# A two-layer metaformer kernel: the experts of group g+2 issued ahead of the second experts of group g, stages spread over more slots, and the weight broadcast cut into four pieces

## What is computed

```python
x = x + L0_conv(_ln_c(x), ...)     # state-space mixer of one image
t = t + L0_ffn(_ln_t(t), ...)      # 8 experts, hidden 128, top 2
x = x + L1_conv(_ln_c(x), ...)     # divisive normalisation, 3x3 taps + channel mix
t = t + L1_ffn(_ln_t(t), ...)      # 8 experts, hidden 256, top 2
```

## Time and profile before

| | |
|---|---|
| median of 3 runs | 746.52 us (745.37 to 746.63) |
| profiled execution | 745.84 us, of which the span is 744.1 us and 1.7 us lie around it |
| busy: TensorE matmul (PE) | 566.3 us, 76% of the span |
| weight load (PEld) | 276.6 us, 37% |
| VectorE (DVE) | 437.4 us, 59% |
| ScalarE (ACT) | 372.7 us, 50% |
| GpSimd (POOL) | 245.7 us, 33% |
| chain that ended last | PE 40%, DVE 27%, ACT 11%, DMA 8%, issue 7%, POOL 6% |

### The profile page before, as it was taken

The page is one execution under the profiler, slowest core; times in us unless marked ns, Lnnn a source line. Parts: engine busy times, 40 slices in busy tenths (PEclk is TensorE's granted clock), DMA queues, the critical chain, the costliest instruction groups (busy, mean ns, idle before and its releaser), DMA issues.

```text
span 744.1 us, 10005 instructions
## 1 busy us (share of the span) xinstructions
PE 566.3 (76%) x3778; PEld 276.6 (37%) x3778; DVE 437.4 (59%) x810; ACT 372.7 (50%) x454; POOL 245.7 (33%) x217
## 2 busy tenths in 40 slices
PE   2645675579868995999768986998589968976677
PEld 1242253325423442445224532454244523432333
DVE  3255347454777569574967487756865495546412
ACT  2214322565446655575548554764557564644432
POOL 2020243122523344342442342434434243423103
PEclk9999875799989999899989998999899997989688
DMA  4501400515014500641052401450055005320140
GB/s 66 101 0 43 87 0 0 109 35 104 1 32 98 116 0 15 130 90 27 15 112 52 83 14 49 82 116 1 17 114 114 3 15 115 85 46 0 25 91 28
DMA packets 27838, 41.47 MB, mean 56 GB/s; under 512 B 11792, under 2 KB 19088, under 8 KB 27792
## 3 DMA queue, kind: packets, MB, share of 16 engines
q1 hardware_dynamic: 27152, 38.75, 25.4%
q0 software_dynamic: 640, 2.10, 0.9%
HBM read 38.22 MB, written 2.62 MB: 55 GB/s over the span
## 4 chain that ended last, share of the span: by engine, by line
PE 40%; DVE 27%; ACT 11%; DMA 8%; issue 7%; POOL 6%; SPq 1%; POOLq 0%; DVEq 0%; ACTq 0%
PE yP L863 11%; PE hP L847 11%; DMA WB<-w_scratch 6%; DVE nacc L1149 4%; PE sA L773 3%; PE sA L786 3%; PE sA L780 2%; PE sC L876 2%; ACT H L690 2%; ACT L574 2%; POOL stat_b L494 2%; DVE xsplit L979 2%; DVE xnrm L976 2%; DVE xcen_b L976 2%; PE sA L759 2%
## 5 line engine op out<-in xcount | busy, mean ns | idle before, releaser
L690 ACT ACTIVATE H<-hP,b 128x1024 f32<-128x1024 f32 x192 | 211.0, 1113 | 111.1 <-PE hP L847 108.4
L863 PE MATMUL yP<-H,w 128*64 128x512 f32 x768 | 208.9, 626 | 21.9 <-DVE ACC L1193 14.3
L847 PE MATMUL hP<-xT,w 128*64 128x512 f16 x1536 | 215.7, 406 | 10.6 <-ACT H L690 10.5
L552 POOL TENSOR_TENSOR ACC<-ACC,YW 128x512 f32<-128x512 f32 x96 | 125.4, 1310 | 212.6 <-DVE YW L1193 212.5
L847 PEld LDWEIGHTS hP<-xT,w 128*64 128x64 f16 x1536 | 83.2, 115 | 139.0 <-issue 74.1
L1193 DVE SCALAR_TENSOR_TENSOR YW<-yP,b,WB 128x512 f32<-128x512 f32 x96 | 71.4, 744 | 30.2 <-PE yP L863 30.1
L863 PEld LDWEIGHTS yP<-H,w 128*64 128x64 f32 x768 | 54.1, 143 | 61.7 <-issue 30.6
L1149 DVE SCALAR_TENSOR_TENSOR nacc<-PAD,taps,nacc 128x528 f32<-128x528 f32 x56 | 52.7, 941 | 1.7
L1193 DVE SCALAR_TENSOR_TENSOR ACC<-yP,b,WB 128x512 f32<-128x512 f32 x32 | 23.1, 745 | 41.7 <-DMA WB<-w_scratch 41.7
L1207 DVE TENSOR_TENSOR X<-sC,X 128x256 f32<-128x256 f32 x32 | 13.5, 423 | 53.9 <-PE sC L876 53.9
L876 PEld LDWEIGHTS sC<-fold,ACC 128*128 128x128 f32 x256 | 32.4, 198 | 25.6 <-issue 19.1
(11 more groups left out here) (144 smaller groups left out, 728.4 us busy)
## 6 DMA issues: line engine op xcount, KB each, us to landing
WB<-w_scratch SPq DMA_DIRECT2D x32, 1024.0 KB, 10.1
X<-in_x SPq DMA_DIRECT2D x8, 256.0 KB, 12.0
out<-X POOLq DMA_DIRECT2D x8, 256.0 KB, 2.8
H<-in_L_ffn_W SPq DMA_DIRECT2D x2, 512.0 KB, 6.7
H<-in_L_ffn_W SPq DMA_DIRECT2D x2, 256.0 KB, 4.2
w<-in_L_ffn_W SPq DMA_DIRECT2D x1, 512.0 KB, 5.2
w_scratch<-wTs SPq DMA_DIRECT2D x16, 32.0 KB, 1.8
w<-in_L_ffn_W SPq DMA_DIRECT2D x1, 256.0 KB, 4.4
```

Of the source, the lines that this page charges most:

```text
L552: pool.tensor_tensor(ACC[l][:, cols], ACC[l][:, cols], YW[:, u % 4, :], ALU.add).then_inc(summed, 1)
L690: nc.scalar.activation(H[:, s % RING, :], hP[s % 2][:, :], ACT.Gelu, bias=b1[l][:, e * ch + c:e * ch + c + 1], scale=1.0 / WS)\
L847: mm = nc.tensor.matmul(hP[s % 2][b * C:(b + 1) * C, hf * HALF:(hf + 1) * HALF], w1[l][:, sp, w, b * C:(b + 1) * C], xT[l][g % 2][:, hf * ...
L863: mm = nc.tensor.matmul(yP[hf][a * C:(a + 1) * C, :], w2[l][:, (2 * j + a) * ch + c, :], H[:, (2 * ch * j + 2 * c + a) % RING, hf * HALF:( ...
```

## The change

- Moe(0, g) moves 24 slots ahead of where it stood relative to moe(1, g): a round is now moe(0, g+2) and moe(1, g). Before the rounds there are two stretches of 24 slots with first experts alone. The last two groups' second experts follow one another without first experts between them.
- The cd steps are spread over more slots (`turn_d` from 15 to 20, `send` from 19 to 25), and all start two slots later after their moe(0, g). The ab tables keep their numbers.
- `X3` gets a third buffer. Moe(1, 6) accumulates in `ACC0` instead of `ACC1`.
- The read of the weights is cut into four pieces, one for each expert pair, of two transfers of 256 KB, each with its own semaphore. A piece waits only for the units of that pair in the previous group. For the second experts the pieces are issued in slots of their own. VectorE waits for a pair's piece ahead of each pair.

```diff
+DEPTH = 2
 PE_AT = dict(
-    cd=dict(turn_c=4, pool0=4, turn_u=11, turn_d=15, gate=16, send=19),
-    final=(12, 14, 24, 26))
+    cd=dict(turn_c=5, pool0=6, turn_u=13, turn_d=20, gate=22, send=25),
+    final=(13, 16, 24, 26))
 ...
 def moe_start(layer, g):
-    return SLOTS * (g - 1) if layer == 0 else SLOTS * g + E
+    if layer == 0:
+        return SLOTS * (g - DEPTH)
+    if g + DEPTH < GROUPS:
+        return SLOTS * g + E
+    return moe_start(1, g - 1) + E * CHUNKS[1]
 ...
 def cd_start(g):
-    return moe_start(0, g) + E * CHUNKS[0] + LAG + 2
+    return moe_start(0, g) + E * CHUNKS[0] + LAG + 4
 ...
+            def spread_piece(l, g, j):
                 if g >= 1:
-                    sp.wait_ge(scaled, 8 * (POS[(l, g - 1)] + 1))
+                    sp.wait_ge(scaled, 8 * POS[(l, g - 1)] + 2 * j + 2)
                 for a in range(2):
-                    src = scratch[l][i].rearrange("(j a) n -> a j n", a=2)[a]
-                    sp.dma_start(WB[l][a * C:a * C + C, :, :], src.partition_broadcast(C)).then_inc(w_in[l][i], 16)
+                    sp.dma_start(WB[l][a * C:a * C + C, j, :],
+                                 scratch[l][g % 2][2 * j + a:2 * j + a + 1, :].partition_broadcast(C)
+                                 .rearrange("c a n -> c (a n)")).then_inc(w_in[l][j], 16)
 ...
                 if k == "send":
                     spread_weights(1, g)
+                    spread_piece(1, g, 0)
+                elif k in ("piece1", "piece2", "piece3"):
+                    spread_piece(1, g, int(k[-1]))
```

More of the change, by code:

```diff
@@ L63 @@
             sums_b=30, turn_b=31, top2=35, send=36),
-    cd=dict(sums_c=1, turn_c=4, norms=9, sums_d=11, turn_d=14, top2=17, send=18),
+    cd=dict(sums_c=1, turn_c=5, norms=11, sums_d=16, turn_d=20, top2=23, send=25),
     final=NO_FINAL)
@@ L68 @@
             centre_b=29, sums_b=30, norm_b=31, top2=35, weights=35),
-    cd=dict(centre_c=1, sums_c=1, norm_c=3, pool0=5, pool1=6, pool2=7, pool3=7, turn_u=10, centre_d=10,
-            sums_d=12, norm_d=14, top2=17, weights=18),
-    final=(12, 13, 24, 27))
+    cd=dict(centre_c=0, sums_c=1, norm_c=3, pool0=7, pool1=8, pool2=9, pool3=10, turn_u=14, centre_d=15,
+            sums_d=16, norm_d=18, top2=23, weights=24),
+    final=(13, 16, 24, 26))
 POOL_AT = dict(
     ab=dict(sums_a=7, norm_a=9, state=26, y_sums=28, sums_b=29),
-    cd=dict(sums_c=1, norm_c=2, scale=8, sums_d=12),
+    cd=dict(sums_c=1, norm_c=2, scale=12, sums_d=16),
     final=NO_FINAL)
@@ L77 @@
     ab=dict(decay=22, send=35),
-    cd=dict(send=21),
+    cd=dict(send=26, piece1=30, piece2=34, piece3=38),
     final=NO_FINAL)
@@ L136, in build_metaformer @@
         n += E * CHUNKS[m[0]]
+    ACC_OF = {m: 0 if m[0] == 0 or GROUPS - m[1] in range(2, DEPTH + 1) else 1 for m in ORDER}
+    ACC_BEFORE = {}
+    for i in range(2):
+        users = [m for m in ORDER if ACC_OF[m] == i]
+        ACC_BEFORE.update(zip(users[1:], users))
     with ExitStack() as ctx:
@@ L193, in build_metaformer @@
         X2b = sb("X2b", [P, T, C])
-        X3 = [sb(f"X3_{i}", [P, T, C]) for i in range(2)]
+        X3 = [sb(f"X3_{i}", [P, T, C]) for i in range(3)]
         X4 = [sb(f"X4_{i}", [P, T, C]) for i in range(2)]
@@ L281, in build_metaformer @@
         w_out = [[sem(f"w_out{l}_{i}") for i in range(2)] for l in range(2)]
-        w_in = [[sem(f"w_in{l}_{i}") for i in range(2)] for l in range(2)]
+        w_in = [[sem(f"w_in{l}_{j}") for j in range(PAIRS)] for l in range(2)]
         x2b = count("x2b", 1)
@@ L457, in ab @@
                     spread_weights(0, g)
+                    for j in range(PAIRS):
+                        spread_piece(0, g, j)
             def cd(g, k):
```

24 lines of the change are left out of this document (12 added, 12 removed).

## The result

The changed kernel takes 756.20 us in the median of four runs (755.18 to 757.23); the kernel before, on the same chip, 745.94 (742.31 to 746.63). The ratio is 1.0159, with a 95% interval from 1.0123 to 1.0196. The profiled execution took 755.29 us, of which the span is 753.5. I had forecast 739 and a gain.

The account below looks back on a forecast made before the run. TensorE was taken as the nearest bound, with 13.3 us of waits a round. The terms 66.7 + 58 + 70 + 407 + 55 + 80 gave a span of 737 us, and with run overhead 739 us, range 718 to 757.

Parts of the forecast that it names:

- the full round: Round of moe(0, g+2) and moe(1, g): 80.4 us less 7.2 saved plus 8.2 new, so 81.4 us.
- second stretch: Stretch with moe(0, 0) alone: shrinks from 68.61 to 58 us, mainly because the first weight piece lands 7 us earlier.
- the two last parts: After the full rounds: 24 slots with moe(0, 7) and moe(1, 5), 55 us; moe(1, 6), moe(1, 7) and the end, 80.
- what goes: Waits removed or shortened in a full round at yP, `mix`, `turn_d` and `send`: 7.2 us saved.
- The third stretch: New 24 slots with moe(0, 1) beside ab(2) and half of cd(0): 70 us, between 62 and 76.
- the wait is 4.1 instead of 1.54: At `turn_b` in a full round: only three slots remain after `mix_out`, adding 2.6 us of wait.
- Ahead of `Vs` now stand a `final` half and layer norm d, 144.30 to 146.18, 1.9 us: At `state` in a full round: TensorE waits 2.4 us for `Vs` instead of 0.57, adding 1.9.
- so +1.9 more: Behind the `turn_b` wait in a full round: TensorE runs at 1.2 GHz, costing 1.9 us more.
- The break-even: Round length R at which 329.7 + 5R equals the old span: 82.9 us, against 81.4 forecast.
- The third rival: In a full round, six taps become late and TensorE waits at `turn_u`: R = 86, 762 us; chance 0.22.
- The second: Rival at the start: weight pieces land no earlier, second stretch stays at 68, time 751 us; chance 0.08.
- The table loads: On ScalarE: twelve more loads of 1.28 us, some 2 us a round, counted only within the `turn_u` wait.

Follow-up runs that it names:

- runs with filled waits: Changed kernel plus matmuls with overwritten product ahead of the waits at `state` and `turn_b`: 734.25 us; with ten more at `send`: 725.89 us.
- the depth alone: Changed kernel with the cd and `final` tables of before, keeping two groups of depth and the four weight pieces: 727.07 us, ratio 0.9809.
- mixed tables: Changed kernel with old places for `turn_c`, channel mix and first taps, later ones for the rest, layer norm d behind `Vs`: 738.34 us, ratio 0.9944.
- depth and filled `send`: Changed kernel with the old cd and `final` tables, plus 23 matmuls with overwritten product in the wait at `send`: 717.01 us, ratio 0.9647.
- the filled `send`: Kernel before with only the four weight pieces, plus 23 matmuls with overwritten product in the wait at `send`: 709.09 us, ratio 0.9542.

## Why the prediction was wrong

**The direction failed on one term, the full round.** The parts, forecast and measured: second stretch 58 and 62.5, third 70 and 69.7, five rounds 407 and 422.4, the two last parts 55 + 80 and 54.8 + 77.5. The differences are +4.5, -0.3, +15.4 and -2.7; together 16.8, which is the span of 753.5 less the 736.7 that the terms of the forecast add up to. I had written that the round decides, from R = 82.9 on; it is 84.5 in the mean. The time of 756.2 lies just inside the stated range, on the side to which I gave a chance of 0.30.

**Right in the round:** what goes. No wait is left at `mix`, `turn_d` or the yP block for `YW`; `send` waits 2.69 us where I said 2.8. `turn_u` waits 1.89 (1.8 forecast) for `zT`. Gone are 7.3 us, where I had 7.2.

**The third stretch came out right by luck.** I built it as 58 for the nearest stretch and 12 of additions. The nearest stretch measured 62.5, so the additions were 7.2: two errors of some 4.5 us cancel.

**Wrong in size: the step "the wait is 4.1 instead of 1.54" at `turn_b`.** It is 5.21. I took the chain of before and gave it back 0.9 us, without asking what GpSimd does beside it in the new order. One VectorE row was held by an `ACC` addition before as well; now `X2b` runs there too and the two hold two rows. Moving `X2b` away gave back 0.95 us, nearly the whole of the error of 1.1.

**Wrong in size: the step "Ahead of `Vs` now stand a `final` half and layer norm d, 144.30 to 146.18, 1.9 us" at `state`.** The wait is 4.22 us instead of 2.4. The rows were the right ones, but I took their price of 1.9 us from the stretch with first experts alone, where GpSimd adds nothing beside them. In the full round before, the same three rows took 3.9 us (307.69 to 311.58), as they do in the changed kernel (394.02 to 397.90). These 2.0 us more cover the whole error of 1.8. Moving layer norm d away brought the wait to 2.45, not to 0.57; the two `zdt` rows then took 2.0 us more beside GpSimd's additions.

**Wrong in kind: the step "so +1.9 more", one stretch at 1.2 GHz.** I priced the clock behind `turn_b` only. It falls behind `state` in every round too, and behind `turn_u` in two of the five. TensorE's busy time in the full round shown rose by 4.6 us (67.06 to 71.68), its idle time by 0.9 (13.3 to 14.2): 80.39 + 0.9 + 4.6 = 85.9. My terms had +1.9 and -0.9. So of the 4.5 us by which this round is longer than forecast, 2.7 are the clock and 1.8 the waits (the 1.1 + 1.8 mis-sized, less small waits that went). The runs with filled waits show it on the whole kernel: 2.7% of the time, some 20 us, comes back from work that does nothing but keep TensorE running.

**The break-even was drawn in the wrong place for the same reason.** I compared waits taken away with waits added and one slow stretch, 7.2 against 8.2. But the 5.74 us wait at `send` had one slow stretch behind it and still has it at 2.69 us; the waits of 1.2 to 1.6 that went had none. Halving a long wait saved its half and no clock; spreading the time over `turn_u`, `state` and `turn_b` bought two or three further slow stretches a round. The third rival came nearest by its round (R = 86, 762 us), but not by its mechanism: `turn_u` stayed at 1.89 us, far under the 3.3 from which the taps would decide. The second lies as near by its time (751 us), and the first piece, which by it would land no earlier, let `ACC` start 7.5 us earlier.

**The pieces:** right in mechanism and small in size. The first `ACC` row of the changed kernel starts at 74.98 us (75.5 forecast, 82.49 before). Alone, the pieces shorten the second stretch by 7.3 us. The changed order then lengthened it by 1.2 instead of shortening it by 1.2: `send` waits 3.89 us there instead of 7.63, but `turn_b` 9.56 instead of 3.84. And of VectorE's ten waits for `WB` I had priced the first alone, 15.92 of 41.7 us; the pieces are worth some 22 us in all.

**The table loads:** 57 as the order of the programs said, 1,283 ns each. One stands in the chain to `turn_u`, at 373.79 us ahead of `norms`, and was in its forecast; no run takes the twelve away, so an effect of their own is not shown. ScalarE is busy 49.48 us of a round of 85.86.

**On the port** the trace goes further than I used the page. `xnrm` and `xcen_b` take 1.75 us beside GpSimd's additions instead of 0.69, and the casts behind them 1.37 instead of 0.43. The Trainium skill (SBUF — State Buffer, "Who interferes with whom") names both kinds: VectorE instructions with two inputs in SBUF, and casts. The trace agrees with both. I applied the rule to the taps, where I looked for trouble, and not to the two layer norms.

What stays open: why the depth alone costs about 1% (0.9705 to 0.9809 without fillers, 0.9542 to 0.9647 with them, so it is not the clock behind `send`). The profiled executions show where it lies. They differ by 2.6 us only (spans of 719.6 and 722.2). The rounds are as long with the depth as without (78.5 and 78.7 us in the mean), while the third stretch and the end take 65.8 + 135.7 us, against 119.8 for the end and 78.7 for one more round without the depth: 2.9 us more. With `send` filled the same sums are 203.9 and 196.7 us. Why one execution has 3 us and the other 7 is not shown. Open too is what decides whether the lower clock follows a wait of 2 to 3 us.

## What to carry to other kernels

Count a wait of the tensor engine twice: its length, and the matmuls behind it that run at half clock. Where a long wait can't be removed, keep it in one piece rather than spread it over several places: here 12.3 us in five waits lost against 12.1 with one long one. Or fill it with matmuls whose product nobody reads; that was worth 12 us here on a kernel of 721. When a step moves, look up what GpSimd does at the new place and price the step's VectorE rows with that beside them. Here a full round of the old trace had the right price, 3.9 us, and the stretch from which it was read had half of it. And measure the parts of a change apart: this one held a gain of 3% inside a loss of 1.6%.

## What the runs showed of the hardware

- A wait of two or three microseconds is followed by the lower clock at one time and not at another. After 2.45 us at `state` the next H block took 1.92 us in the kernel with layer norm d moved and 1.05 in the one with mixed tables. After 2.69 us at `send` the yP block took 1.98 us in the changed kernel, and after 2.68 us 1.08 with `state` and `turn_b` filled. After some 1.9 us at `turn_u` the changed kernel shows 1.92 in the round above and 1.05 in the round behind it:

```profile
463.55 0.71 PE L839 MATMUL sC<-ident,zT 128*128 128x128 f32 x4 [1.90 <-POOL zT L554]
...
464.63 1.05 PE L866 MATMUL hP<-xT,w 128*64 128x512 f16 x8
```

- The run times of one kernel can spread with the clock: ten runs of the mixed tables lie from 734.75 to 745.10 us, and the four near 735 have a granted clock of 0.894 to 0.900, the three near 745 one of 0.881. That many such waits cause it is not shown: the four runs of the changed kernel lie within 2.1 us, and so do the four of the kernel with depth and filled `send`.
- The mean granted clock of a span does not rank kernels: 0.925 goes with the span of 722.2 us of the old tables with depth and with the 707.5 us of the filled `send`. The rows behind each wait show where the slow stretches fall.
- GpSimd's additions of two 128x512 tiles hold some VectorE rows beside them, short ones too: rows of 0.69, 0.43 and 0.22 us took 1.75, 1.37 and 1.28 us. The same row's price therefore depends on its place in the order.
